# Row sums issued one tile later on TensorE, and an earlier first load of the gate/up weights, in a two-sublayer block on eight cores

## What is computed

```python
def _layernorm(x, axis=-1, eps=1e-5):
    m = jnp.mean(x, axis=axis, keepdims=True)
    v = jnp.var(x, axis=axis, keepdims=True)
    return (x - m) / jnp.sqrt(v + eps)

# attention-like sublayer: x (4, 2048, 2048), 16 states
x_proj = x @ proj_in_w.T + proj_in_b
delta = softplus(x_proj @ B_w.T)
h_t = h_{t-1} * sigmoid(A) + x_t[:, :, None] * d_t[:, None, :]
y_t = h_t.sum(axis=1) @ C_w.T + D_param * x_t
y = y @ proj_out_w.T + proj_out_b + x

# feed-forward sublayer: 2048 -> 8192 -> 2048, int8 weights
fuse = silu((x @ w_gate) * s_gate) * ((x @ w_up) * s_up)
y = (fuse @ w_down) * s_down

x = x + layernorm(attention(layernorm(x)))
x = x + layernorm(feed_forward(layernorm(x)))
```

## Time and profile before

| what | value |
|---|---|
| median of 2 runs | 2319.49 us (2319.13 to 2319.85) |
| profiled execution, its own time | 2317.57 us |
| span of the profiled execution, slowest core (core 4) | 2316.0 us |
| spans of the eight cores | 2307.9 to 2316.0 us |
| TensorE busy with matmuls | 1822.8 us, 79% of the span |
| VectorE, ScalarE, GpSimd busy | 390.3, 349.3, 153.4 us |
| mean granted TensorE clock, by core | 0.908 to 0.929 |

### The profile page before, as it was taken

One profiled execution on the slowest core, in us unless ns is written; L12 is line 12 of the kernel. 1 busy time (PEld: TensorE's weight loads), 2 busy tenths in 40 slices (PEclk: granted clock), 3 DMA queues, 4 the chain that ended last, 5 costly groups with the idle time before them and its releaser, 6 DMA issues.

```text
span 2316.0 us, 20962 instructions; the slowest of 8 cores (2307.9 to 2316.0 us)
## 1 busy us (share of the span) xinstructions
PE 1822.8 (79%) x8229; PEld 761.7 (33%) x8229; DVE 390.3 (17%) x653; ACT 349.3 (15%) x590; POOL 153.4 (7%) x294
## 2 busy tenths in 40 slices
PE   1519986577743699999998888789999999788880
PEld 0004432122200244444443333334444444333330
DVE  3260013200056411111110000031111111500005
ACT  4602201312134110010110000000100101000000
POOL 0000000000000000000001111100000000011110
PEclk9999997699965799999999999989999999899995
DMA  6003300122200244443442333334434443533332
GB/s 179 0 0 65 63 1 1 28 39 43 37 0 1 93 161 146 153 156 146 178 150 100 118 126 120 111 116 149 160 146 156 153 145 134 175 126 119 121 107 73
DMA packets 53428, 237.23 MB, mean 102 GB/s; under 512 B 7859, under 2 KB 8244, under 8 KB 36948
## 3 DMA queue, kind: packets, MB, share of 16 engines
q0 software_dynamic: 41648, 218.25, 28.5%
q1 hardware_dynamic: 11684, 17.64, 2.3%
HBM read 143.73 MB, written 8.39 MB: 66 GB/s over the span
## 4 chain that ended last, share of the span: by engine, by line
PE 71%; DVE 10%; ACT 8%; DMA 6%; issue 4%; DVEq 0%; ACTq 0%; SPq 0%; POOLq 0%
PE pb L218 71%; DMA WRDBT<-wd_t 3%; DMA WRDAT<-wd_t 3%; DVE SQTT L546 1%; DVE SQTT L878 1%; ACT SQTT L732 1%; ACT SQTT L745 1%; ACT SQTT L987 1%; ACT SCRT L691 1%; DVE YPRE L697 1%; DVE XN1T L549 1%; DVE XPBT L738 1%; ACT SQTT L465 1%; DVE SCRT L787 1%; DVE XT L790 1%
## 5 line engine op out<-in xcount | busy, mean ns | idle before, releaser
L218 PE MATMUL pb<-X2NAT,WGUA 128*128 128x512 bf16 x2048 | 449.8, 382 | 18.4 <-DVE X2NAT L882 18.4
L218 PE MATMUL pb<-X2NBT,WGUB 128*128 128x512 bf16 x2048 | 448.8, 381 | 15.2 <-DVE X2NBT L882 14.7
L218 PEld LDWEIGHTS pb<-X2NAT,WGUA 128*128 128x128 bf16 x2048 | 200.7, 98 | 267.5 <-issue 29.6
L218 PEld LDWEIGHTS pb<-X2NBT,WGUB 128*128 128x128 bf16 x2048 | 200.8, 98 | 263.3 <-issue 24.9
L218 PE MATMUL pb<-FUSETB,WRDBT 128*128 128x512 bf16 x1024 | 232.0, 385 | 21.3 <-DMA WRDBT<-wd_t 21.2
L218 PE MATMUL pb<-FUSETA,WRDAT 128*128 128x512 bf16 x1024 | 227.1, 379 | 15.0 <-DMA WRDAT<-wd_t 13.6
L916 ACT ACTIVATE SCRT<-pb,SGC 128x512 f32<-128x512 f32 x128 | 88.0, 687 | 828.4 <-PE pb L218 828.4
L218 PE MATMUL pb<-SQTT,ONESB 128*1 128x512 bf16 (+1 forms) x224 | 93.5, 490 | 133.4 <-ACT SQTT L467 55.9
L218 PE MATMUL pb<-XN1T,WRIT 128*128 128x512 bf16 (+1 forms) x768 | 121.3, 321 | 35.5 <-DVE XN1T L549 35.3
L218 PEld LDWEIGHTS pb<-FUSETB,WRDBT 128*128 128x128 bf16 x1024 | 98.1, 99 | 154.3 <-issue 47.0
L218 PEld LDWEIGHTS pb<-FUSETA,WRDAT 128*128 128x128 bf16 x1024 | 96.9, 98 | 144.4 <-issue 34.7
(11 more groups left out here) (103 smaller groups left out, 759.2 us busy)
## 6 DMA issues: line engine op xcount, KB each, us to landing
WGUA<-wgu_t POOLq DMA_DIRECT2D x64, 1024.0 KB, 4.9
WGUB<-wgu_t POOLq DMA_DIRECT2D x64, 1024.0 KB, 4.9
WRDAT<-wd_t POOLq DMA_DIRECT2D x64, 512.0 KB, 3.4
WRDBT<-wd_t POOLq DMA_DIRECT2D x64, 512.0 KB, 3.4
WRIT<-w_in_t POOLq DMA_DIRECT2D x16, 512.0 KB, 6.2
XT<-xT SPq DMA_DIRECT2D x2, 4096.0 KB, 26.8
WROT<-w_out_t POOLq DMA_DIRECT2D x16, 512.0 KB, 5.8
out_xT<-XT SPq DMA_DIRECT2D x2, 4096.0 KB, 15.1
```

What stands on the lines that cost most here:

```text
L218: e.matmul(o, l, r, start=st, stop=sp))
```

## The change

The two matmuls of a pair of sums are put into a function `pend_sum`, which is called after the main matmuls of the next tile, so that the pair of tile n follows the matmuls of tile n + 1 on TensorE. This is done in the output projection and in the down projection. After each loop one last call issues the last pair. Apart from that, loads of gate/up weights move: for k = 0 both are issued right after the output projection, in place of after layer norm 2; for k = 1 the first is issued at the end of the gate/up loop of k = 0, into slot 1 of WGUB, and only the second stays where it was. The slots of k = 1 are counted from 1 for that.

```diff
-    o_wguB = al.pin(167936, 2 * 8192, 8, 11, "wguB")
+    o_wguB = al.pin(167936, 8192, 8, 11, "wguB_s0")
+    al.pin(176128, 8192, 7, 11, "wguB_s1")
...
+    pend_sum = None
     for t in range(DT):
...
             bk.w_pe = t_pe.n
+            if pend_sum is not None:
+                pend_sum()
             sl = (t * 2 + wi) % 2
...
-            W("tensor", t_vec, vv)
-            bsum = 6 if wi == 0 else 7
-            bsq = 4 if wi == 0 else 5
-            mm(pb[bsum][0:1, 0:512], ONESB, YATT(t, l0, l0 + 512),
-               t == 0, t == DT - 1)
-            W("tensor", t_scl, vsq)
-            sq_prev[sl] = mm(pb[bsq][0:1, 0:512], ONESB, SQT(2 + sl)[:, 0:512],
-                             t == 0, t == DT - 1)
+
+            def pend_sum(t=t, wi=wi, l0=l0, sl=sl, vv=vv, vsq=vsq):
+                W("tensor", t_vec, vv)
+                mm(pb[6 if wi == 0 else 7][0:1, 0:512], ONESB,
+                   YATT(t, l0, l0 + 512), t == 0, t == DT - 1)
+                W("tensor", t_scl, vsq)
+                sq_prev[sl] = mm(pb[4 if wi == 0 else 5][0:1, 0:512], ONESB,
+                                 SQT(2 + sl)[:, 0:512], t == 0, t == DT - 1)
...
+    pend_sum()
     for b_ in (4, 5, 6, 7):
         banks[b_].w_pe = t_pe.n
+    v_wgu = {}
+    W("gpsimd", t_pe, t_pe.n)
+    for i in range(2):
+        v_wgu[i] = DMA("gpsimd", s_wrf[i % 2],
+                       lambda e, i=i: e.dma_start(out=WGUPW(0, i % 2),
+                                                  in_=d_wgu[i]))
...
-        W("gpsimd", t_pe, t_pe.n)
-        for i in range(2):
-            v_wgu[i] = DMA("gpsimd", s_wrf[i % 2],
-                           lambda e, i=i, k=k: e.dma_start(out=WGUPW(k, i % 2),
-                                                           in_=d_wgu[i]))
+        slg = (lambda i: i % 2) if k == 0 else (lambda i: (i + 1) % 2)
+        if k == 0:
+            pass
+        else:
+            v_wgu[0] = v_wgu_k1
+            W("gpsimd", t_pe, t_pe.n)
+            v_wgu[1] = DMA("gpsimd", s_wrf[0],
+                           lambda e: e.dma_start(out=WGUPW(1, 0),
+                                                 in_=d_wgu[1]))
...
+        if k == 0:
+            W("gpsimd", t_pe, t_pe.n)
+            v_wgu_k1 = DMA("gpsimd", s_wrf[1],
+                           lambda e: e.dma_start(out=WGUPW(1, 1),
+                                                 in_=d_wgu[0]))
...
             bk.w_pe = t_pe.n
+            if pend_sum is not None:
+                pend_sum()
             sl = t % 2
...
-            W("tensor", t_scl, vsc)
-            mm(pb[6 if k == 0 else 7][0:1, 0:512], ONESB, Y2W(k, t),
-               t == 0, t == DT - 1)
-            sqd_prev[sl] = mm(pb[0 if k == 0 else 1][0:1, 0:512], ONESB,
-                              SQT(sl)[:, 0:512], t == 0, t == DT - 1)
+
+            def pend_sum(t=t, k=k, sl=sl, vsc=vsc):
+                W("tensor", t_scl, vsc)
+                mm(pb[6 if k == 0 else 7][0:1, 0:512], ONESB, Y2W(k, t),
+                   t == 0, t == DT - 1)
+                sqd_prev[sl] = mm(pb[0 if k == 0 else 1][0:1, 0:512], ONESB,
+                                  SQT(sl)[:, 0:512], t == 0, t == DT - 1)
+        pend_sum()
```

More of the change, by code:

```diff
@@ L858, in emit_final @@
                       ba=ba, bb=bb)
-    v_wgu = {}
     v_wd = {}
@@ L902, in build_program @@
                 mm(pb[bg.idx][:, 0:512],
-                   WGUPW(k, i % 2)[:, j * 128:(j + 1) * 128],
+                   WGUPW(k, slg(i))[:, j * 128:(j + 1) * 128],
                    X2NW(k, j), j == 0, j == DT - 1)
@@ L907, in build_program @@
                 mm(pb[bu.idx][:, 0:512],
-                   WGUPW(k, i % 2)[:, 2048 + j * 128:2048 + (j + 1) * 128],
+                   WGUPW(k, slg(i))[:, 2048 + j * 128:2048 + (j + 1) * 128],
                    X2NW(k, j), j == 0, j == DT - 1)
@@ L929, in build_program @@
                 W("gpsimd", t_pe, t_pe.n)
-                v_wgu[i + 2] = DMA("gpsimd", s_wrf[i % 2],
-                                   lambda e, i=i, k=k: e.dma_start(
-                                       out=WGUPW(k, i % 2), in_=d_wgu[i + 2]))
+                v_wgu[i + 2] = DMA("gpsimd", s_wrf[slg(i)],
+                                   lambda e, i=i, k=k, s=slg(i): e.dma_start(
+                                       out=WGUPW(k, s), in_=d_wgu[i + 2]))
             if i == 48 and k == 0:
```

## The result

The changed kernel is faster: the ratio to the kernel before is 0.9436, with a 95% interval of 0.9383 to 0.9489. On the 2319.49 us shown before that is 2188.7 us (2176 to 2201 by the interval); 2188 was predicted. The profiled execution of the changed kernel took 2193.1 us, its slowest core (core 7) has a span of 2191.6 us, and the eight spans are 2184.6 to 2191.6 us.

The account below looks back on a forecast made before the run. TensorE was the engine to follow, standing still for VectorE's add, ScalarE's squares and down-weight loads. Gains of 87.9 and 43.2 us less 1.0 make 130.1, taking 2317.6 to 2187.5, stated as a median of 2188; range 2170 to 2212.

Parts of the forecast that it names:

- Output projection: Output projection loop: 219.0 us falls to 131.1, 87.9 less, of which 59.4 waits, 18.6 clock and 9.9 matmul draining.
- the pair: Pair of sums between output projection groups: waits for nothing and costs 0.52 us, 16.1 us for 31 pairs.
- WROT's refills: Output projection weight refills: 6.7 us left for landing, taken as 6.2, so cost nothing; upper bound 21 us.
- Down projections: Down projection loops: loads bound a tile at 15.38 us against 16.92; 23.1 less 1.5 a pass, 43.2 us in both.
- the 15.4 to 15.6 that were to be seen: Sign of being right: down projection evictions lie 15.4 to 15.6 us apart.
- late loads: Down projections: excess of 5.4 and 13.6 us over regular tiles is kept, plus 1.5 us a pass, bounds 0 and 5.
- Moved loads: Gate/up weight loads: no gain, and 1 us lost to a WGUB load ahead of WRDAT's refills; bounds 0 and 1.7.
- Loads that land later as they come more often: Rival, down projections: 4.29 us from issue to matmul instead of 3.52, no gain there, 2231 us; chance 0.10.
- Clock: Rival, output projection: clock doesn't stay at 1.00, slow stretches or dense work cost 19 us, 2207 us; chance 0.10.
- Loads that hide: Rival, down projections: loads land fast enough, 14.34 us a tile, 31 us less, 2157 us; chance 0.04.
- Slots in each other's way: Rival, down projections: back-to-back loads slow each other; 5.7 us a load eats all gain, 6.6 gives 2373; chance 0.02.
- no effect: Rival, both loops: another wait holds the pair or the group behind it, time stays near 2318 us; chance 0.02.

Follow-up runs that it names:

- ring of four: The changed kernel with four slots instead of two for the down weights, refilled for the same quarter of the next tile: ratio 0.9215 to the kernel before, median 2139.3 us.

## Why the prediction was right

**The number.** That 2188.7 lies 0.7 us from the forecast is luck; the interval is 12 us to either side. By stages, on the two cores shown, the gain was 126.0 us where 130.1 was predicted: 3.0 less in the output projection, 2.1 less in the down projections, and the 1 us charged for the moved loads didn't come.

**Output projection.** Predicted 131.1 us and a gain of 87.9; measured 134.1 and 84.9. The mechanism held in each point: the pair waits for nothing, the clock stays up, and WROT's refills are hidden. These land after 5.1 us (median) where 6.2 was taken from the input projection, and no matmul behind the first waits for one. The term that was off is the pair. I priced it at 0.52 us from a place where it stood behind a pause. In a dense stream the step from the last main matmul to the pair costs 0.10 us more: a group's first matmul is at 472.63 and the sum at 476.18, 3.55 us later, not 3.455. At 31 groups that is the missing 3 us. In the old trace a wait stood at this place, so the step couldn't be read there.

**Down projections.** Predicted gain 21.6 us a pass; measured 19.1 and 22.0 on the cores shown and 20.4 and 21.0 as means of the eight. That the loads would take the place of the pauses was the step that mattered: without it the forecast would have been a tile of 14.34, 31 us faster. The ring of four showed it. A regular tile came out as predicted, 1219.86 - 1204.37 = 15.49 us for 15.38, with the pair of sums in the time in which the next load lands:

```profile
1204.37 7.23 PE L219 MATMUL pb<-FUSETA,WRDAT 128*128 128x512 bf16 x32
...
1212.09 7.21 PE L219 MATMUL pb<-FUSETA,WRDAT 128*128 128x512 bf16 x32 [0.49 <-DMA WRDAT<-wd_t]
...
1219.23 0.38 PE L219 MATMUL pb<-Y2AT,ONESB 128*1 128x512 bf16 x1
...
1219.86 7.32 PE L219 MATMUL pb<-FUSETA,WRDAT 128*128 128x512 bf16 x32
```

The average tile of that core is 16.0 us (240.1 / 15), above the 15.4 to 15.6 that were to be seen, because late loads are the rest. Predicted were 5.4 + 1.5 = 6.9 us of them in the first pass; core 7 has 9.4 and the mean of the eight cores 7.5. The usual landing of 3.38 us was a little short for what ends a wait: on core 7 the 27 landings in the chain of the first pass average 3.7 us, and the 16 in the chain before averaged 3.6.

**Moved loads.** Predicted 1 us lost. No run resolves 1 us: with the moved loads the two down projections together are 0.9 us longer than without (means of eight cores), and the time shows nothing in either direction. The load of WGUB ahead of WRDAT's refills did not delay the first of them: it is issued at 1143.79 and its matmuls start at 1147.36, 3.57 us later, where 3.52 is usual.

```profile
1138.74 0.53 POOL L972 DMA_DIRECT2D WGUB<-wgu_t  x1 [13.29 <-PE pb L219]
...
1143.79 0.53 POOL L995 DMA_DIRECT2D WRDAT<-wd_t  x1 [4.52 <-PE pb L219]
...
1147.36 7.07 PE L219 MATMUL pb<-FUSETA,WRDAT 128*128 128x512 bf16 x32 [0.67 <-DMA WRDAT<-wd_t]
```

**The rivals.** Loads that land later as they come more often: their median went from 3.4 to 3.5 us, and 4.29 from issue to matmul would have eaten the gain. The Trainium skill says that HBM latency grows with load (DMA: Bandwidth & Descriptors, "Latency and other measured facts"). The sign agrees and the size is small: with the ring of four the loads come more often still, and their medians are 3.4 to 3.6 us. Clock: it is 0.99 in the output projection of core 7 and 1.00 in gate/up on all eight cores. The Trainium skill expects a reduced clock with all cores dense (TensorE: Matmul & The Clock Gate, "Seeing it yourself"), and this execution doesn't show it. Loads that hide: no regular tile is near 14.34, and 58 waits for them are left. Slots in each other's way would have needed a landing some 2 us longer to eat the gain, and no effect would have left the time at 2318; neither came.

## What to carry to other kernels

When a dense engine waits for a neighbour's result that only a side product needs, put the side product one tile later; count the gain as the waits and also as the clock that the pauses cost. By the rows before, these were 59 and 19 us here, of the 85 gained. Before counting it, work out the next bound in the same loop, here the cycle of a two-slot ring: compute of a slot, issue, landing. If that cycle is longer than the work of two slots, the deferral gives only the difference between the old period and the cycle, here 42 us in place of 55, and deepening the ring belongs to the same change. And a load moved earlier was worth nothing here, because another engine's tiles came last.

## What was not expected of the hardware

A switch between 128-column weights and the one-column weights of the sums costs about 0.1 us each way in a dense stream: a pair of 512-column matmuls takes 0.62 us of TensorE, where two plain ones take 0.43. It isn't the change of PSUM bank, since gate/up changes its bank every sixteen matmuls and keeps to 216 ns. It isn't the semaphore wait either, since quarters of the down projection with a wait for their slot follow each other at the plain 216 ns in the ring of four. The timeline of that kernel, four quarters in a row:

```profile
1852.36 7.07 PE L219 MATMUL pb<-FUSETB,WREBT 128*128 128x512 bf16 x32
...
1859.26 7.07 PE L219 MATMUL pb<-FUSETB,WRDBT 128*128 128x512 bf16 x32
```

From 1852.36 to 1859.26 are 6.90 us for 32 matmuls. What the 0.1 us is spent on, no run here tells.
